# First graph convolution: the batch's own rows scaled on VectorE in one product, not on ScalarE in four

## What is computed

```python
def _gcn_conv(x, W, b, src, dst, dinv, n_nodes):
    h = x @ W
    norm = dinv[src] * dinv[dst]
    msgs = h[src] * norm[:, None]
    out = jax.ops.segment_sum(msgs, dst, num_segments=n_nodes)
    return out + b

# src, dst here hold the edges and a loop from every node to itself
deg = jax.ops.segment_sum(jnp.ones_like(dst, dtype=x.dtype), dst, num_segments=n_nodes)
dinv = jnp.where(deg > 0, jax.lax.rsqrt(jnp.maximum(deg, 1e-12)), 0.0)
h = jax.nn.relu(_gcn_conv(x, W1, b1, src, dst, dinv, n_nodes))
out = _gcn_conv(h, W2, b2, src, dst, dinv, n_nodes)
```

## Time and profile before

| what | value |
|---|---|
| time, median of 3 runs | 3194.56 us (3194.03 to 3195.92) |
| the profiled execution's own time | 3193.83 us |
| its span, first to last instruction | 3192.1 us |
| mean granted TensorE clock over the span | 0.855 of full speed |
| first convolution, first gather to the last before the next stage | 538.66 to 872.18 us |
| first gather of the next stage | 910.20 us |
| VectorE, ScalarE, GpSimd, TensorE busy over the span | 73%, 54%, 66%, 72% |

### The profile page before, as it was taken

How to read it: one execution, slowest core, us unless ns; L and a number is a source line. 1 busy time by engine, 2 the same in 40 slices (tenths; PEclk the granted TensorE clock), 3 DMA queues, 4 the chain that set the end, 5 groups by cost and what they waited for, 6 DMA issues and landing times. The chain is left out here.

```text
span 3192.1 us, 53001 instructions
## 1 busy us (share of the span) xinstructions
PE 2304.3 (72%) x9863; PEld 1472.6 (46%) x9864; DVE 2341.2 (73%) x7354; ACT 1716.2 (54%) x4736; POOL 2103.6 (66%) x2070
## 2 busy tenths in 40 slices
PE   2766664777746666599999576577645499999996
PEld 1444443666645556344444333366534355444442
DVE  7998864788858888599999211134488678899996
ACT  1776776788947777466666344455458512121221
POOL 1777774777747777477776677577540277677775
PEclk9998887999978887799999789755555599999998
DMA  1666554455536665355554577799745423222221
GB/s 48 212 214 198 181 176 146 147 166 174 177 102 190 185 193 184 121 148 150 151 159 145 182 265 260 225 289 288 225 127 174 137 71 73 61 60 62 62 62 38
DMA packets 320170, 497.00 MB, mean 156 GB/s; under 512 B 65930, under 2 KB 144681, under 8 KB 320058
## 3 DMA queue, kind: packets, MB, share of 16 engines
q1 hardware_dynamic: 251130, 379.68, 36.9%
q0 software_dynamic: 68928, 116.12, 13.8%
HBM read 262.91 MB, written 236.52 MB: 156 GB/s over the span
## 5 line engine op out<-in xcount | busy, mean ns | idle before, releaser
L2152 PE MATMUL bank<-sum_masked,sum_w 128*128 128x512 f32 x1280 | 567.7, 595 | 6.7 <-DVE sum_masked L2211 6.7
L2211 DVE SCALAR_TENSOR_TENSOR sum_masked<-sum_typ,sum_col 128x512 f32<-128x512 bf16 x640 | 401.6, 685 | 19.9 <-ACT sum_col L2127 17.1
L1378 PE MATMUL bank<-mean_masked,mean_w 128*128 128x512 f32 x784 | 376.9, 611 | 18.0 <-DVE mean_masked L1468 18.0
L2152 PEld LDWEIGHTS bank<-sum_masked,sum_w 128*128 128x128 f32 x1280 | 236.2, 191 | 280.7 <-issue 209.3
L2071 POOL DMA_INDIRECT sum_rows<-t_x,m_row_int x160 | 167.8, 1049 | 200.3 <-POOLq L122 151.8
L1234 POOL DMA_INDIRECT mean_rows<-t_x,m_row_int x196 | 219.4, 1119 | 94.1 <-issue 59.4
L2093 POOL DMA_INDIRECT out_dram<-sum_new,m_last_int x196 | 221.4, 1130 | 90.0 <-issue 58.0
L1468 DVE SCALAR_TENSOR_TENSOR mean_masked<-mean_typ,mean_col 128x512 f32<-128x512 bf16 x392 | 249.8, 679 | 19.1 <-ACT mean_col L1314 19.0
L1694 POOL DMA_INDIRECT at_xs<-t_x,at_order x204 | 193.3, 948 | 94.4 <-issue 61.3
L1234 POOL DMA_INDIRECT c_rows<-x_dram,m_src_int x196 | 188.9, 964 | 98.0 <-issue 55.4
L1234 POOL DMA_INDIRECT c_rows<-t_g,m_row_int x196 | 188.4, 961 | 96.5 <-issue 57.0
(11 more groups left out here) (366 smaller groups left out, 6039.1 us busy)
## 6 DMA issues: line engine op xcount, KB each, us to landing
t_hu<-at_made SPq DMA_DIRECT2D x51, 512.0 KB
pf_xc<-x_dram SPq DMA_DIRECT2D x98, 256.0 KB, 3.0
t_g<-pf_g SPq DMA_DIRECT2D x98, 256.0 KB
t_x<-pf_x SPq DMA_DIRECT2D x98, 256.0 KB
c_dense_x<-t_x SPq DMA_DIRECT2D x98, 256.0 KB, 3.8
t_x<-c_dense_x SPq DMA_DIRECT2D x98, 256.0 KB
c_same<-p_same SPq DMA_DIRECT2D x98, 128.0 KB, 3.5
t_g<-c_new SPq DMA_DIRECT2D x49, 256.0 KB
```

The costliest lines, as they stand in the source:

```text
L1378: pe.matmul(H[q][:, :], w[:, r, :], masked[:, r % MASKS, :], start=(r == 0), stop=(r == n_rel - 1))\
L2152: pe.matmul(H[n % 2][:, :], w[:, r * D:(r + 1) * D], masked[:, r % 8, :], start=(r == 0), stop=(r == R16 - 1)).then_inc(mask_used, 1)
L2211: v.scalar_tensor_tensor(out=masked[:, r % 8, :], in0=typ[:, n % 2, :], scalar=float(r), in1=col[:, n % 2, :], op0=ALU.is_equal, op1=ALU.m ...
```

## The change

The four ScalarE operations that make `own` are removed. VectorE makes it instead, with one product of the whole batch (512 elements in each partition) and `self_col`, each value of which is repeated 128 times by a step of zero (`bc`). The product stands in VectorE's body for batch b + 1, behind the norms and ahead of `add_b2`. It waits until TensorE has used the slot two batches ago (`turned`). The wait for `self_col` moves from ScalarE to VectorE and is met once, ahead of the first body.

```diff
         @block.scalar
         def _(act):
-            if kind == CONV1:
-                act.wait_ge(self_ready, 1)
...
                     last.then_inc(scaled_ready, 1)
-                    if kind == CONV1:
-                        for j in range(BT):
-                            last = act.activation(own[:, o, j, :], xd_of(s, j), ACT.Copy,
-                                                  scale=self_col[:, bass.ds(s * BT + j, 1)])
-                        last.then_inc(own_ready, 1)
...
                 v.tensor_tensor(self_col[:, :], squares[:, :], m.ends_col[:, :], ALU.mult).then_inc(self_ready, 1)
+                v.wait_ge(self_ready, 1)
...
+            def own_rows(s, q):
+
+                if not runs(s, 0, LAST):
+                    return
+                if runs(s, 2):
+                    v.wait_ge(turned, s - 1)
+                v.tensor_tensor(own[:, q], wide(xd_at(s)), bc(at(self_col, s), D), ALU.mult).then_inc(own_ready, 1)
...
                     if kind == CONV1:
                         norms(b + 2)
+                        own_rows(b + 1, o)
                         add_b2(b - 4, q)
                     scan(b - 1, o)
```

## The result

The changed kernel takes 3199.94 us (median of 19 runs, 3195.08 to 3202.33) against 3194.56 us before (median of 19 runs); the ratio of the means is 1.0015, with a 95% interval from 1.0008 to 1.0022. That is +4.8 us (the medians differ by 5.4), from +2.6 to +7.0. The middle is inside what was called no change (up to 6.4 us), and the interval reaches a little past its slow edge. The forecast was 3197.6 us, +3.

The account below looks back on a forecast made before the run. The ring (6.84 us a body) bounded the kernel, GpSimd (6.75) close behind; VectorE would take over at 7.01. Stretch +5.5, ends -2.8, delays under 1: total +3 on 3194.56, so 3197.6 us, range 3191 to 3208.

Parts of the forecast that it names:

- The ring: First convolution's cycle of ScalarE scalings and TensorE matmuls: sets today's pace, 6.84 us a body, falling to 5.67.
- VectorE's own pace: VectorE's time a body in the even stretch without its slack waiting for c_new: 6.40 us, 7.01 with the product.
- The product's price: VectorE time the added 128x512 product takes in each body: 0.61 us, bounded by 0.47 and 0.75.
- Rival 3: Level or faster: VectorE's pauses at the loop's head take in the product, GpSimd sets the pace; 3191 us, chance 0.1.
- The ends: Head and tail of the first convolution stage, where the ring sets the pace: together shorter by 2.8 us.
- The head: Start of the stage: the first c_new comes 1.17 us earlier, so -1.2 us.
- The tail: Last bodies of the stage: savings of 0.2, 0.3 and 1.1 us until VectorE already set the pace.
- GpSimd, the step that was mis-sized: GpSimd's gather pace in the even stretch: 6.75 us a body, 6.9 if hindrance by VectorE products doubles, still under VectorE.
- Rival 1: Slower: GpSimd held through both touching VectorE products becomes the bound at 7.21 us a body; 3205 us, chance 0.2.
- its sign for rival 1: In the changed profile, ScalarE waiting for gathers and VectorE waiting again, with GpSimd issues of up to 2.1 us.
- The term for delays: VectorE and GpSimd hindering each other: at most 0.02 us a body, under 1 us in the stretch.
- TensorE's waits: In the changed kernel, TensorE waits for c_scaled and never for c_own, which is ready over a microsecond earlier.

Follow-up runs that it names:

- both_engines: Kernel before, keeping its four ScalarE operations, plus the VectorE product at the change's place into a tile nobody reads; ratio to before 1.0031.
- own_left_out: Kernel before with no own rows made in the batches on either engine (own set to zero once ahead of the stage); ratio to before 0.9976.
- own_behind_scan: Changed kernel with the VectorE product moved behind the scan, apart from c_biased; ratio to before 1.0020.
- own_half: Changed kernel with two of the four own tiles made on ScalarE and two in one VectorE product; ratio to before 1.0008.
- own_at_end: Changed kernel with the VectorE product at the end of VectorE's body, one body earlier; ratios to before 0.9983 and 0.9989 in two samples.
- info_early: Changed kernel with all gathers of info moved to the stage before; whole time not comparable, stretch of 39 bodies 274.2 us.

## Why the prediction was right, point by point

**The ring and what stands behind it.** Right. The ring lost its 1.17 us and the even bodies gained nothing from it; both_engines, with the ring whole, runs them as fast.

**VectorE's own pace, 6.40 us, from the pause ahead of L1547 and not from the busy share.** Right: 6.39, and with the product 7.00 to 7.01 against the 7.01 of the sum. That part gives +5.0 us in the stretch against +5.5.

**The product's price, 0.61 us.** Right where the change puts it (7.00 - 6.39 = 0.61, or 0.60 before rounding), by both_engines too. But it is no property of the operation: 0.33 us at the end of the body, 0.42 in the middle, and half the product costs 0.48 at the place of the change. Rival 3, which said that pauses could take the product in, named the mechanism and rightly excluded it for this place, since the pauses lie ahead of it; even so, the change made the head's pause longer, 0.59 instead of 0.49.

**The ends, -2.8 us.** The head gave -0.9 and -1.0 in the two traces against -1.2. The tail gave -1.3 and -0.6 against -1.6. Together that is 2.2 and 1.6 us less. The prediction had called it a sign of being wrong if they did not shrink by some 3 us; they shrank by about half to three quarters of that.

**GpSimd, the step that was mis-sized.** The prediction put 6.75 us for its pace, and 6.9 us with the hindrance doubled, which is 0.2 to 0.3 us of hindrance. The runs showed 0.42 to 0.44 us in the changed kernel, and a pace of 6.86 with one product only (own_left_out). Chance meeting of issues and products, which the estimate assumed, is not what happens: the issues lock to the products. In the last 31 bodies of the stretch of the changed kernel the first issue behind the start of `c_own` begins 0.65, 0.15, 0.13 and 0.87 us after it, or within 0.03 us of that, over and over (once 1.13 in place of 0.87). Rival 1 came nearer to the size (0.55) from a wrong mechanism. An issue is never held through both products. GpSimd's pace came to 7.0 to 7.1 us, level with VectorE's, so its issues used up their lead and gathers came late; its sign for rival 1, ScalarE waiting for gathers, did appear. The term for delays, put at 0.3 us, was 2.7 us of VectorE's waiting in one trace and 0.8 in the other, and 2.57 of the 2.7 are TensorE at its lower clock behind a late gather. That GpSimd's pace came out level with VectorE's and not above it is what kept the time near the forecast, and the estimate of 0.2 to 0.3 us did not secure it: in own_behind_scan the same work in another order made GpSimd the limit. To that extent the forecast had luck.

Together: 5.0 - 0.9 - 1.3 + 2.7 = +5.5 us in the first trace, and 5.4 - 1.0 - 0.6 + 0.8 = +4.6 in the second; the forecast was +3, and the measured ratio means +4.8. The sign, the size and the engine that sets the pace were right; the ends and the delays were off by 0.5 to 2.4 us, both towards slower.

**TensorE's waits.** It never waited for `c_own`, as said, but it waited for the scan too, which was not said. That its clock would fall was not foreseen either. In most bodies that cost nothing, since VectorE did not wait for it; in the one body with the long wait it cost nearly all of the 2.7 us.

## What to carry to other kernels

Before you move work to an engine whose busy share looks low, work out its own pace: the period less the pauses in which it truly waits for another engine. Pauses that the profile puts down to issue were no room for more work here, unless a long operation was placed just ahead of them; the same product cost 0.60 or 0.33 us by its place alone, and this decided between slower and faster. And once the tight ring is gone, ask how the runner-up behaves when nothing spaces it any more.

## What the runs showed of the hardware

- A GpSimd gather issue that begins in the first half microsecond of a VectorE operation with two SBUF sources (128x512 f32, 0.69 us) is let go 0.53 to 0.58 us after that operation began (one case of over 300 took 0.79), and it then takes its normal 0.94 us. The longest such issue took 1.47 us, so the delay is at most 0.53 us in these stretches; no issue was held across two operations that touch. In own_half the operation is half as long (128x256, 0.43 us), and the issue is let go 0.30 us after its start. The Trainium skill, "SBUF — State Buffer", section "SBUF: two separate sides", has this as a lock held for the whole instruction; the traces agree in kind, and put the release some 0.1 us ahead of the recorded end.
- The four short operations of `add_product` (128x128) hindered an issue by up to 0.17 us in these stretches.
- Issues and products lock in phase, so the mean delay is no matter of chance: 0.42 and 0.44 us a body in two traces of the changed kernel, 0.17 and 0.18 in two of own_at_end, and 0.17 to 0.56 over the five arrangements that have the whole product on VectorE alone. Why a given placement locks where it does was not settled.
- TensorE's granted clock over the stretch was 0.99 to 1.00 where its pauses were regular (1.7 to 2.4 us ahead of each batch), and 0.91 to 0.96 where they varied, at the same number of matmuls. The longest pause does not tell the two apart: it was 2.4 us in info_early, at 0.96, as in both_engines, at 0.99. No run isolated this.
